# Causal attention: value products two groups of scores behind, four buffers of exponentials, value rows of 16 columns

## What is computed

```python
qkv = x @ w_attn                                   # x is layer-normed
q, k = (t.reshape(B, T, 2 * H, 4).transpose(0, 2, 1, 3) for t in (q, k))   # 32 score heads of 4 columns
v = v.reshape(B, T, H, 8).transpose(0, 2, 1, 3)    # 16 value heads of 8 columns
att = softmax(where(causal, q @ k.T, -inf))        # B, 32, T, T with T = 1024
att = att.reshape(B, H, 2, T, T)
att = att[:, :, 0] - lambda_full * att[:, :, 1]
out = att @ v                                      # then an RMS norm per head, and w_proj
```

## Time and profile before

| what | value |
|---|---|
| median of three runs | 2081.5 us |
| the profiled execution: its time, its span | 2084.54 us, 2082.5 us |
| busy over the span: TensorE, VectorE, ScalarE, GpSimd | 1836.3, 1875.1, 1120.8, 1395.1 us |
| mean granted TensorE clock | 0.957 of full speed |
| score matmuls (L517), count and busy time | 768, 215.2 us |
| value matmuls (L530), count and busy time | 1536, 164.7 us |
| maxima on VectorE (L589), count and busy time | 384, 354.9 us |

### The profile page before, as it was taken

The page is one execution under the profiler, slowest core; times in us unless marked ns, Lnnn a source line. Parts: engine busy times, 40 slices in busy tenths (PEclk is TensorE's granted clock), DMA queues, the critical chain, the costliest instruction groups (busy, mean ns, idle before and its releaser), DMA issues. The chain is left out here.

```text
span 2082.5 us, 35441 instructions
## 1 busy us (share of the span) xinstructions
PE 1836.3 (88%) x14080; PEld 1359.7 (65%) x14080; DVE 1875.1 (90%) x1681; ACT 1120.8 (54%) x1469; POOL 1395.1 (67%) x655
## 2 busy tenths in 40 slices
PE   3899999999856989889898998988989989899886
PEld 2344444444243777769777787877877878778785
DVE  7887887887266999999999999999999999999994
ACT  3376777676612455455554555555455554555552
POOL 5122222222201989989889898898988989989890
PEclk8899999999965999999999999999999999999996
DMA  3300000000000000000000000000000000000000
GB/s 105 65 6 8 9 7 8 9 5 1 1 1 0 1 1 1 1 1 1 1 1 2 1 1 2 1 1 2 1 1 1 2 1 1 2 1 1 1 1 20
DMA packets 11094, 14.28 MB, mean 7 GB/s; under 512 B 4672, under 2 KB 7776, under 8 KB 10816
## 3 DMA queue, kind: packets, MB, share of 16 engines
q1 hardware_dynamic: 9216, 8.91, 2.0%
q10 hardware_dynamic: 1728, 3.12, 0.4%
HBM read 4.65 MB, written 1.05 MB: 3 GB/s over the span
## 5 line engine op out<-in xcount | busy, mean ns | idle before, releaser
L1065 POOL TENSOR_TENSOR b_p_ring<-b_p_ring,b_m 128x2048 f32<-128x2048 f32 (+7 forms) x384 | 1249.5, 3300 | 198.8 <-DVE b_p_ring L979 196.8
L1101 ACT ACTIVATE b_p_ring<-b_p_ring 128x2048 f32<-128x2048 f32 (+7 forms) x384 | 532.8, 1412 | 640.7 <-POOL b_p_ring L1065 640.0
L1167 PE MATMUL b_ps<-k_ident,b_ev_ring 128*128 128x128 f32 (+6 forms) x4608 | 581.0, 276 | 100.8 <-DVE b_ev_ring L1025 100.7
L1025 DVE TENSOR_TENSOR b_ev_ring<-b_p_ring,b_ps 128x2048 f32<-128x2048 f32 (+7 forms) x384 | 636.9, 1663 | 1.5 <-ACT b_p_ring L1101 1.3
L979 DVE TENSOR_TENSOR b_p_ring<-b_ps,b_key 128x2048 f32<-128x2048 f32 (+7 forms) x384 | 636.8, 1666 | 0.0
L1167 PE MATMUL b_ps<-k_ident,b_p_ring 128*128 128x128 f32 (+6 forms) x4608 | 578.6, 276 | 33.3 <-issue 22.2
L1167 PEld LDWEIGHTS b_ps<-k_ident,b_ev_ring 128*128 128x128 f32 (+6 forms) x4608 | 496.3, 136 | 155.5 <-DVE b_ev_ring L1025 131.4
L1167 PEld LDWEIGHTS b_ps<-k_ident,b_p_ring 128*128 128x128 f32 (+6 forms) x4608 | 512.9, 137 | 41.6 <-issue 25.1
L589 DVE TENSOR_REDUCE a_negm<-a_ps 128x1 f32<-128x768 f32 (+7 forms) x384 | 354.9, 955 | 90.0 <-PE a_ps L478 88.6
L572 ACT ACTIVATE a_ex<-a_ps 128x512 f32<-128x512 f32 (+3 forms) x768 | 334.2, 498 | 176.6 <-PE a_ps L517 174.9
L408 POOL TENSOR_SCALAR_AFFINE_SELECT a_ex<-a_ex 128x512 f32<-128x512 f32 x128 | 81.2, 635 | 365.1 <-ACT a_ex L572 365.0
(11 more groups left out here) (174 smaller groups left out, 981.1 us busy)
## 6 DMA issues: line engine op xcount, KB each, us to landing
rk_of_group<-rows_k SPq DMA_DIRECT2D x96, 32.0 KB, 1.9
rq<-rows_q SPq DMA_DIRECT2D x42, 64.0 KB, 2.4
k_wqkv<-in_wqkv ACTq DMA_DIRECT2D x1, 2048.0 KB, 10.3
out<-x_all SPq DMA_DIRECT2D x4, 256.0 KB, 2.3
k_wo<-in_wo ACTq DMA_DIRECT2D x1, 512.0 KB, 10.3
rq<-rows_q SPq DMA_DIRECT2D x12, 32.0 KB, 2.0
k_w_attn<-in_w_attn ACTq DMA_DIRECT2D x1, 192.0 KB, 3.1
k_reset_min<-in_reset_min ACTq DMA_DIRECT2D x1, 128.0 KB, 10.4
```

Of the source, the lines that this page charges most:

```text
L1025: nc.vector.tensor_tensor(chunk(ev_ring, c), chunk(p_ring, c), over_queries(values(c), c), ALU.mult).then_inc(ev_done.sem, 1)
L1065: nc.gpsimd.tensor_tensor(pc, pc, over_rows(m[:, half].rearrange("p i h -> p (i h)"), c), ALU.subtract).then_inc(shifted.sem, 1)
L1101: nc.scalar.activation(pc, pc, ACT.Exp).then_inc(exp_done.sem, 1)
L1167: last = nc.tensor.matmul(ps[0:width, bank, b // IB * P:(b // IB + 1) * P], rows[:, r, b:hi].rearrange("p i h -> p (i h)"), k["ident"][:], ...
```

## The change

The values of a group are given two groups of scores later instead of one (`LAG`), the exponentials have four buffers instead of three (`EX_SLOTS`), and the places that depend on it move along: the turn may come from group 3 on, `combine` stands behind the mask of group 3, the copies of O one group later. The value rows have 16 columns per head (8 values, the ones, 7 zeros), with one more row of zeros and a one at the end; the stationary operand is still 32 columns, so that a head's operand now holds the next head's columns too, whose sums are not read.

```diff
+    EX_SLOTS, LAG = 4, 2
...
-        ex = sb("ex", [P, 3, 4, 512])
+        ex = sb("ex", [P, EX_SLOTS, 4, 512])
...
-                    if at == 2 and n >= 1:
+                    if at == 3 and n >= 1:
                         combine(n - 1)
...
-                                            v1[:, b * NT + sbk, 2 * g + hh // 2, :], ex[:, (G * n + at) % 3, hh, 0:hi - lo],
+                                            v1[:, b * NT + sbk, 2 * g + hh // 2:2 * g + hh // 2 + 2, :].rearrange("p n c -> p (n c)"), ex[:, (G * n + at) % EX_SLOTS, hh, 0:hi - lo],
...
-                            if todo[given][0] == "turn" and at < 2:
+                            if todo[given][0] == "turn" and at < 1 + LAG:
                                 break
...
-                    if at >= 1:
-                        values(n, at - 1)
+                    if at >= LAG:
+                        values(n, at - LAG)
                     elif n >= 1:
-                        values(n - 1, G - 1)
-            values(JOBS - 1, G - 1)
+                        values(n - 1, G + at - LAG)
+            for at in range(G - LAG, G):
+                values(JOBS - 1, at)
...
-                        if G * n + at >= 3 and hh == 0:
-                            act.wait_ge(values_done.sem, G * n + at - 2)
+                        if G * n + at >= EX_SLOTS and hh == 0:
+                            act.wait_ge(values_done.sem, G * n + at - EX_SLOTS + 1)
...
-                    if at == 0 and n >= 1:
+                    if at == LAG - 1 and n >= 1:
                         copy_o(n - 1, 1)
-                    if at == 4:
+                    if at == 3 + LAG:
                         copy_o(n, 0)
...
-        v1 = sb_a("v1", [P, TILES, GROUPS * 2, 32])
+        v1 = sb_a("v1", [P, TILES, GROUPS * 2 + 1, 2 * A_V])
```

More of the change, by code:

```diff
@@ L244, in _ @@
                 act.wait_ge(qkv_psum.sem, 3 * s + 3)
-                nc.scalar.copy(v1[:, piece(s), :, 0:A_V], ps_v[:].rearrange("p (n v c) -> p n v c", n=FT, c=A_V)).then_inc(qkv_taken.sem, 1)
+                nc.scalar.copy(v1[:, piece(s), 0:GROUPS * 2, 0:A_V], ps_v[:].rearrange("p (n v c) -> p n v c", n=FT, c=A_V)).then_inc(qkv_taken.sem, 1)
             act.wait_ge(const_step.sem, 3)
@@ L406, in mask @@
                 pool.wait_ge(exp_done.sem, exp_done.at(n, 4 * at + 4))
-                block_diagonal = ex[:, (G * n + at) % 3, :, 0:P]
+                block_diagonal = ex[:, (G * n + at) % EX_SLOTS, :, 0:P]
                 nc.gpsimd.affine_select(block_diagonal, block_diagonal, [[0, 4], [1, P]], ALU.is_ge, 0.0, base=0,
@@ L568, in _ @@
                         act.wait_ge(st_psum.sem, s + 1)
-                        if G * n + at >= 3 and hh == 0:
-                            act.wait_ge(values_done.sem, G * n + at - 2)
+                        if G * n + at >= EX_SLOTS and hh == 0:
+                            act.wait_ge(values_done.sem, G * n + at - EX_SLOTS + 1)
                         lo, hi = queries_of(half, sbk)
-                        nc.scalar.activation(ex[:, (G * n + at) % 3, hh, 0:hi - lo], ps[:, ST_BANK + s % ST_SLOTS, 0:hi - lo],
+                        nc.scalar.activation(ex[:, (G * n + at) % EX_SLOTS, hh, 0:hi - lo], ps[:, ST_BANK + s % ST_SLOTS, 0:hi - lo],
                                              ACT.Exp).then_inc(exp_done.sem, 1)
-                    if at == 0 and n >= 1:
+                    if at == LAG - 1 and n >= 1:
                         copy_o(n - 1, 1)
-                    if at == 4:
+                    if at == 3 + LAG:
                         copy_o(n, 0)
```

## The result

The changed kernel takes **2089.25 us** (median of 10 runs, 2084.92 to 2090.46), the one before 2081.9 (10 runs, 2077.36 to 2083.8): a ratio of 1.0031, interval 1.0022 to 1.0041, so slower by 4.6 to 8.5 us. Forecast were 2087.4 us (2083.0 to 2091.0) and 0.75 for slower. The profiled execution took 2089.2 us, its span is 2087.3.

The account below looks back on a forecast made before the run. TensorE's in-order queue was taken as the bound, with VectorE the limit between division and 314.4 us in a job. Thirteen jobs' +10.4, job 14's -4.2 and job 15's -0.3 made +5.9 us: 2087.4 us, range 2083.0 to 2091.0.

Parts of the forecast that it names:

- Piece A: Job's start to the turn: 0.69 us later, from a 256-query value block (0.64) and a 128-query score (0.05).
- Piece B: VectorE from the division on: 0.69 later, less idle time falling 0.51 to 0.16, plus 0.10 for a pad: 0.44 us.
- the stretch: VectorE from 303.92 to 314.4 us in a job, nine maxima and four pads, without idle time; TensorE waits for it.
- Piece C: From the end of the stretch to the next job: a 512-query value block replaces a 256-query one, +0.36 us.
- Job 14: The 0.85 us wait goes, the 3.93 one shortens, last maxima come sooner, the clock stays up: -4.2 us.
- Job 15: Its first 1.0 us, at the low clock before, would run at full clock: -0.3 us; its tail 0.
- rival 1: The clock falls in job 14 as before, so its gains are lost: 2089.0 us, chance 0.15.
- The rest: Outside the jobs' order: fourth buffer, 16-column value rows and shorter memset of v change nothing, 0 us.
- Rival 2: Pads are held for the whole GpSimd op, 0.36 us more in 13 jobs: 2092.1 us, chance 0.10.
- Rival 3: Half of the 0.80 us per job is made good in 13 jobs: 2082.2 us, chance 0.14.
- Rival 4: VectorE absorbs the later turn, jobs 1 to 13 keep 31.15 us, job 14's waits go: 2077.0 us, chance 0.08.

Follow-up runs that it names:

- e2: The change with the turn allowed from group 2 on, as in the kernel before; lag of two, four buffers and 16-column rows stay: 2080.92 us.
- e1: The kernel before with only the turn moved, allowed from group 3 on instead of group 2, lag still one: 2089.77 us.
- e6: The change with GpSimd's combine back behind the mask of group 2 instead of group 3: 2087.57 us.
- e7: The change with the four pads three items sooner (PAD_ITEM 5 for 8): 2091.61 us.
- e9: The change with the turn two maxima later in the order of items (TURN_ITEM 8 for 6): 2078.66 us.
- e3: The kernel before with only four buffers of exponentials and value rows of 16 columns; lag and turn as before: 2081.6 us.
- e4: The change with another item order (EARLY 6, EARLY_ROWS 5, TURN_ITEM 8, PAD_ITEM 6 for 7, 5, 6, 8): 2070.51 us.
- e10: The kernel before, lag one, with the item order of e4 (6, 5, 8, 6 for 7, 5, 6, 8): 2092.91 us.
- e8: The kernel before with the combine behind the mask of group 3 instead of group 2: 2082.03 us.

## Why the prediction was right

The sign, the place and most of the size were right: slower, by about 0.8 us in each of 13 jobs, less 4 us in job 14. That the job came so close, +0.78 for +0.80, is in part luck: a term too small by 0.1 and a term of 0.1 that isn't there. By its steps:

- **No value product waits for a mask in jobs 1 to 13.** Right: of the 3 waits of the earlier trace rows two are in job 14 and the third, 0.59 us at 573.97, in job 15, and e2, which has the lag without the late turn, gains nothing in jobs 1 to 13. That the waits were in job 14 alone overlooked the third.
- **Piece A, the turn 0.69 later.** Measured 0.79 (7.47 against 6.68), e1 0.94 for a forecast of 0.90. Too small by 0.1. A block of 256 queries adds a little more to the queue than the 0.64 of its row: the score behind it starts 0.73 us after the mask matmul ahead of it (302.00 to 302.73 in the change), where 0.06 would part the two without it. The score of 128 queries took 0.07 for 0.05 (306.87 to 306.94). The other 0.05 I can't place.
- **Piece B, idle time from 0.51 to 0.16.** Right to the hundredth; e1 the same, and division to last maximum is shorter by 0.36.
- **Piece B, the pad 0.10 longer by the combine.** Wrong. They met, begun 0.17 us apart, and the pad took 0.48; e6, without the meeting, has the same job. This term is 0, and the sign that was named for it, a first pad of 0.58, failed; with A's 0.1 more the sum came out as forecast by two errors of opposite sign.
- **"Nothing in the stretch can take that back, since no idle time is in it."** Right in its result, too simple in its reason: e7 took one pad of VectorE's work out of the stretch and the job stayed, TensorE being as full there; e9 took two maxima out, which are work of TensorE too, and it fell by 0.66.
- **Piece C, +0.36.** Measured 0.34 to 0.35 (11.36 against 11.02; 11.36 against 11.01 in e2 and e1).
- **A job of +0.80, 13 jobs +10.4.** Measured +0.78 and +10.1.
- **Job 14, -4.2.** Measured -3.94. The waits went as forecast (0.85 gone, 2.01 for "about 2 us"). The 0.5 for the product of the maxima at full clock was not gained: it took 0.61 for 1.06, but the next job's first score then waited 0.82 for VectorE's addition of the rows (L609), and from the product to that score it is 2.38 us now (551.61 to 553.99), 2.43 before. In e2 and e6, where the clock stayed up, it is 2.21, so that the full clock is worth 0.22 there, not 0.5; job 14 gains 4.17 and 4.16 in these two.
- **Job 15, -0.3.** Measured +0.28, since here the clock fell in job 15 for 3.4 us, part of what rival 1 had priced. In e2 and e6, with the same wait of 2.00 us, it did not, and job 15 took 30.19 and 29.74. e2's holds a wait of 0.81 that the change hasn't: its early turn stands there ahead of the copy of O. e6's gain of 0.50 is more than the 0.3; the mask wait of 0.59 in job 15 went with the lag, where the prediction had put its tail at 0.
- **The rest, 0.** Right (e3).

In the stage this makes +6.3 for a forecast of +5.9. The median came out 1.85 above the forecast, inside its own range; e6, whose jobs 1 to 13 are those of the change, gave 2087.57, so what is left lies within the scatter of the runs. Rival 2 falls: no pad was held for the rest of the combine's step. Rival 3 falls, since nothing was made good. Rival 4 needed a job under 31.5 and had 31.92.

## What to carry to other kernels

A longer lag pays only where a row shows the wait that it covers; elsewhere it moves work between stretches of the queue, and each stretch has its own limit. When a lag is changed, the order that was set for the old one has to be set anew: with an order that suits it either lag gave some 10 us against the kernel before, and the order that gave it in the kernel with a lag of two cost 11 in the one with a lag of one, where the combine stood ahead of a mask that the values wait for. Read a change of a few tenths of a per cent in a job that repeats, not in the span.

## What the runs showed of the hardware

Where a pad (VectorE, tensor_scalar, 128x1024 bf16) and the first step of the combine (GpSimd, tensor_scalar, 128x128 f32) overlapped, GpSimd's step was the longer for it each time: 0.79 us in the change, e4, e9 and e10, 0.76 in e7 and 0.85 in e2 and e8, for 0.60. The pad took its 0.48 where it began 0.17 us (the change) or 0.23 us (e2, e8) into that step, and 0.58 to 0.62 where it began within 0.06 us of its start (e4, e9, e10) or ahead of it (e7, where it also met the end of a mask). With a mask the loss went either way: in e10 a pad begun at 310.29 beside the mask of 310.13 took 0.76, the mask its 0.64; in e7 a pad begun at 306.53 took its 0.48, and the mask of 306.75 took 0.75. Rows of e4:

```profile
300.87 0.58 DVE L600 TENSOR_SCALAR rk<-rk_of_group,k_head_rows 128x1024 bf16<-128x1024 bf16 x1 [0.16 <-DVE a_oh L621]
```

```profile
300.81 0.79 POOL L416 TENSOR_SCALAR a_oh<-a_oh,k_lam 128x128 f32<-128x128 f32 x1 [0.15 <-DVE a_oh L621]
```

By the Trainium skill (SBUF — State Buffer, Who interferes with whom) a VectorE tensor_scalar in a two-port mode and a GpSimd instruction shut each other out for a whole instruction. No run here shows that for this pair, nor in which mode the pads run: by the profile, whose spans of GpSimd are rough, both ran at once, and each lost 0.3 us at most. The pad beside the memset of the earlier trace rows comes nearer to it: the memset ended at 44.48 (43.53 + 0.95), and the pad at 44.75 (43.56 + 1.19), still sooner than a whole pad of 0.48 behind it.

The same stall was not always followed by a fall of the granted clock. Ahead of the product of the maxima in job 14 TensorE waited 2.00 to 2.01 us in the change, e2, e4, e6, e7 and e9. Behind it the clock fell to 0.50, for 3.4 us, in the change, e4, e7 and e9; in e2 and e6 it did not, and e6 has TensorE's program of the change. Its window (columns of the earlier trace rows), with the wait that ends at 552.11 in it:

```profile
541.00:560.00 19.00, 15.23 (x115) 5.26 (x115) 8.21 (x7) 12.64 (x32) 5.12 (x12) 1.00 0.00 1
```

What decides between the two was not tried. Of the ten executions of the change the two with the highest mean granted clock, 0.963, are the two fastest, 2084.92 and 2084.94 us.
